# A Mamba mixer and a sorted mixture of experts: the state sums in two chains, the gate in one VectorE product

## What is computed

```python
def step(h, ins):
    d_t, B_t, C_t, u_t = ins
    dA = jnp.exp(d_t[:, :, None] * A)
    h = h * dA + (d_t * u_t)[:, :, None] * B_t[:, None, :]
    y = jnp.einsum('bds,bs->bd', h, C_t)
    return (h, y)
y = ys.transpose(1, 0, 2) + xm * D_ssm
y = y * jax.nn.silu(res)
return y @ out_w.T + out_b
```

## Time and profile before

| | us |
|---|---|
| three runs | 1684.01, 1685.93, 1693.28 |
| median | 1685.93 |
| span of the profiled execution | 1689.5 |
| of that, first product of the first slot to that of the last | 91.8 to 1573.7 |

### The profile page before, as it was taken

The page is one execution under the profiler, slowest core; times in us unless marked ns, Lnnn a source line. Parts: engine busy times, 40 slices in busy tenths (PEclk is TensorE's granted clock), DMA queues, the critical chain, the costliest instruction groups (busy, mean ns, idle before and its releaser), DMA issues. The chain is left out here.

```text
span 1689.5 us, 29263 instructions
## 1 busy us (share of the span) xinstructions
PE 1330.0 (79%) x8754; PEld 1198.4 (71%) x8754; DVE 1379.1 (82%) x2183; ACT 1278.8 (76%) x2660; POOL 572.0 (34%) x617
## 2 busy tenths in 40 slices
PE   7978568878887787878878787887878787568778
PEld 6867457768777686767767676777867676457668
DVE  3367888989888888989889898989889888988732
ACT  3489657978789787978779698878789698549722
POOL 1211423162423426162423536163332523132210
PEclk9988668988999899998999799998999899778889
DMA  7346446675666767676666767675676765455731
GB/s 233 112 95 136 85 83 149 152 169 126 156 158 139 166 142 180 142 170 134 146 159 142 162 146 165 142 179 125 136 175 141 163 148 114 92 129 126 161 88 45
DMA packets 144662, 236.98 MB, mean 140 GB/s; under 512 B 13696, under 2 KB 79488, under 8 KB 144384
## 3 DMA queue, kind: packets, MB, share of 16 engines
q0 software_dynamic: 39424, 132.15, 40.7%
q1 hardware_dynamic: 105088, 102.97, 20.8%
HBM read 92.46 MB, written 25.17 MB: 70 GB/s over the span
## 5 line engine op out<-in xcount | busy, mean ns | idle before, releaser
L1602 POOL DMA_DIRECT2D acc<-G x224 | 204.2, 911 | 855.8 <-DMA acc<-G 422.1
L973 ACT ACTIVATE dA<-delta,A 128x255 f32<-128x255 f32 x1024 | 425.6, 495 | 6.3 <-DVE hs L1344 5.3
L1350 DVE TENSOR_TENSOR_SCAN hs<-dA,b_r 128x512 f32<-128x512 f32 x256 | 297.9, 1202 | 19.9 <-PE b_r L660 12.6
L1363 DVE TENSOR_TENSOR G<-hs,b_r 128x1024 f32<-128x1024 f32 x224 | 272.4, 1216 | 44.8 <-PE b_r L671 34.9
L1344 DVE TENSOR_TENSOR_SCAN hs<-dA,dbu 128x1024 f32<-128x1024 f32 x128 | 292.8, 2287 | 15.1 <-ACT dA L973 8.8
L535 PE MATMUL b_h<-xsT,wst 128*128 128x128 f32 x1680 | 255.5, 301 | 34.4 <-issue 23.3
L535 PEld LDWEIGHTS b_h<-xsT,wst 128*128 128x128 f32 x1680 | 230.5, 212 | 50.7 <-issue 49.0
L547 PE MATMUL b_out<-w2s,hT 128*128 x1680 | 239.0, 289 | 13.5 <-ACT ys L894 9.6
L843 ACT ACT_TABLE_LOAD x182 | 233.5, 1283 | 4.0 <-PEq L1733 0.7
L547 PEld LDWEIGHTS b_out<-w2s,hT 128*128 128x128 f32 x1680 | 219.9, 203 | 18.4 <-issue 17.0
L660 PE MATMUL b_r<-prm,scaled 128*128 128x128 f32 x1024 | 173.5, 300 | 59.7 <-ACT scaled L989 28.8
(11 more groups left out here) (176 smaller groups left out, 1974.3 us busy)
## 6 DMA issues: line engine op xcount, KB each, us to landing
acc<-G POOLq DMA_DIRECT2D x224, 512.0 KB, 4.8
wst<-w_dram SPq DMA_DIRECT2D x242, 256.0 KB, 2.9
xsort<-sorted SPq DMA_DIRECT2D x70, 192.0 KB, 5.2
results<-ys SPq DMA_DIRECT2D x70, 192.0 KB, 3.0
xin<-x_dram SPq DMA_DIRECT2D x8, 256.0 KB
sorted<-ys SPq DMA_DIRECT2D x2, 960.0 KB, 7.3
sorted<-xn,posi POOLq DMA_INDIRECT x112
yk<-results,posi POOLq DMA_INDIRECT x112
```

The costliest lines, as they stand in the source:

```text
L973: last = do(dA[j % 4][:, d, k, 1:], delta[b][:, k, 1:], ACT.Exp, scale=A[:, k, s:s + 1])
L1350: V.tensor_tensor_scan(hs[j % 2][:, d, :, :].rearrange("p h t -> p (h t)"), dA[j % 4][:, d, :, :].rearrange("p h t -> p (h t)"), R[u % 2][ ...
L1363: V.tensor_tensor(to[:, :, :, :], hs[j % 2][:, :, :, :], both(C).unsqueeze(2).broadcast_to([P, DP, HALVES, T]), ALU.mult).then_inc(q_G, 1)
L1602: Q.dma_start(acc[b][:, :, :, :].rearrange("p d h t -> p (d h t)"), G[j % NG][:, :, :, :].rearrange("p d h t -> p (d h t)"), accum_op=ALU. ...
```

## The change

- `acc` gets the products 0, 2, 4 and 6, a new tile `odd` the products 1, 3, 5, 7 and D x. Products 0 and 1 are written by VectorE directly; 2 to 7 go through the ring of three. The even chain (q_even) and the odd chain (q_odd) wait for their own predecessor alone.
- GpSimd gets `skip` (two tensor_scalar of 128 x 256 that make D x, and a DMA that adds them to the first half of `odd`, 256 KB) and the merges `w1` and `w2` of the slot before: three tensor_tensor of 128 x 512. `w2` adds after the last landing twice in series.
- VectorE's gate is one product and waits for `w2`.
- `selr` holds one column for each selector (128 x 24) and the matmul reads it 128 times (a step of zero). It comes with the parameters; the three loads and the three casts of 128 x 1024 are gone, one cast of 128 x 24 remains.
- The lists of all four slots are in a new order on all four engines. In slot 0 TensorE has 14 pieces of an FFN and in slot 1 21, where there were 16 and 19. ScalarE's leaf F11 moves from slot 2 to slot 3.

```diff
+EVEN = (2, 4, 6)
+ODD = ("skip", 3, 5, 7)
...
     "vector": (
-        "b0 s0 g0 s1 gate g1 b2 s2 g2 s3 low b4 g3 delta s4 g4 s5 b6 mask g5 s6 g6 s7 xb g7",
-        "b0 fstats s0 s1 g0 fnorm b2 s2 flog ftop g1 fplace gate g2 s3 b4 xsum g3 un s4 g4 s5 g5 b6 fweights s6 "
-        "g6 low s7 delta g7 fsum",
-        "b0 s0 s1 g0 gate b2 g1 xsum s2 s3 un g2 b4 lx g3 s4 s5 g4 ln b6 low s6 g5 unx delta g6 s7 g7",
-        "b0 fstats s0 s1 fnorm b2 g0 flog ftop g1 fplace s2 g2 s3 gate g3 b4 s4 fweights g4 s5 low g5 b6 delta s6 "
-        "mask g6 s7 g7 xb fsum",
+        "b0 s0 g0 s1 gate b2 g1 s2 s3 low g2 b4 s4 g3 delta g4 s5 g5 b6 mask s6 g6 s7 xb g7",
+        "b0 fstats s0 s1 fnorm b2 g0 s2 flog ftop g1 fplace gate g2 s3 b4 xsum g3 un s4 fweights g4 s5 g5 b6 "
+        "s6 low g6 delta s7 g7 fsum",
+        "b0 s0 s1 g0 gate b2 g1 xsum s2 s3 un g2 b4 g3 lx s4 ln s5 g4 b6 g5 s6 low unx delta g6 s7 g7",
+        "fstats b0 s0 s1 fnorm b2 g0 flog ftop g1 fplace s2 s3 g2 b4 gate s4 fweights g3 g4 s5 g5 low delta "
+        "b6 s6 mask g6 s7 g7 xb fsum",
     ),
     "gpsimd": (
-        "a1 a2 a3 a4 a5 a6 a7",
-        "froot a1 sc0 sc1 sc2 a2 sc3 sc4 fkeep rms a3 sc5 sc6 sc7 rs a4 ga0 ga1 ga2 ga3 a5 ga4 ga5 ga6 ga7 a6 a7",
-        "a1 rms rs a2 a3 lnx rmsx a4 a5 a6 a7",
-        "froot a1 sc0 sc1 sc2 a2 sc3 sc4 fkeep a3 sc5 sc6 sc7 a4 ga0 ga1 ga2 ga3 a5 ga4 ga5 ga6 ga7 a6 a7",
+        "w1 w2 skip a2 a3 a4 a5 a6 a7",
+        "w1 froot w2 skip sc0 sc1 sc2 sc3 rms a2 sc4 sc5 a3 sc6 sc7 ga0 ga1 ga2 ga3 a4 a5 ga4 ga5 ga6 ga7 a6 "
+        "rs fkeep a7",
+        "w1 w2 rms rs skip a2 a3 lnx rmsx a4 a5 a6 a7",
+        "froot w1 w2 skip sc0 sc1 sc2 sc3 sc4 a2 sc5 sc6 a3 a4 ga0 ga1 ga2 sc7 a5 ga3 ga4 fkeep ga5 ga6 ga7 "
+        "a6 a7",
     ),
...
-        selr = sb("selr", [P, len(SELECTED), P], fp32r)
+        selr = sb("selr", [P, len(SELECTED)], fp32r)
...
+            def selector(row):
+                k = SELECTED.index(row)
+                return selr[:, k:k + 1].broadcast_to([P, P])
...
+        def landed(q, j):
+
+            if j in EVEN:
+                return q_even, 16 * (q * len(EVEN) + EVEN.index(j) + 1)
+            return q_odd, 16 * (q * len(ODD) + ODD.index(j) + 1)
...
-                if j:
-                    last = j - NG if j > NG else max(p for p in range(1, NP) if p % NG == j % NG) - (NP - 1)
-                    wait(dve, q_gs, (q * (NP - 1) + last) * 16)
-                to = G[j % NG] if j else acc[i % 2]
+                if j >= 2:
+                    wait(dve, *(landed(q, j - NG) if j - NG >= 2 else landed(q - 1, j - NG + NP - 2)))
+                to = G[(j - 2) % NG] if j >= 2 else (acc, odd)[j][i % 2]
...
             def gate_y(g, i):
                 q, b = 4 * g + i, i % 2
-                dve.wait_ge(q_gs, (q + 1) * (NP - 1) * 16)
+                dve.wait_ge(q_sum, 3 * q + 3)
                 dve.wait_ge(q_res, 2 * q + 2)
                 wait(dve, q_omm, q)
-                V.tensor_tensor(yg[:, :, :], acc[b][:, 0, :, :], acc[b][:, 1, :, :], ALU.add)
-                dve.drain()
-                for k in range(HALVES):
-                    V.scalar_tensor_tensor(out=yg[:, k, :], in0=xm[b][:, k, :], scalar=par("D_ssm")[:, k:k + 1],
-                                           in1=yg[:, k, :], op0=ALU.mult, op1=ALU.add)
-                dve.drain()
-                V.tensor_tensor(yg[:, :, :], yg[:, :, :], sres[b][:, :, :], ALU.mult).then_inc(q_yg, 1)
+                V.tensor_tensor(yg[:, :, :], acc[b][:, 0, :, :], sres[b][:, :, :], ALU.mult).then_inc(q_yg, 1)
...
                 pool.wait_ge(q_G, q * NP + j + 1)
-                wait(pool, q_gs, (q * (NP - 1) + j - 1) * 16)
-                Q.dma_start(acc[b][:, :, :, :].rearrange("p d h t -> p (d h t)"),
-                            G[j % NG][:, :, :, :].rearrange("p d h t -> p (d h t)"),
-                            accum_op=ALU.add).then_inc(q_gs, 16)
+                if j in EVEN:
+                    wait(pool, *(landed(q, j - 2) if j > 2 else landed(q - 1, 6)))
+                    Q.dma_start(flat(acc[b]), flat(G[(j - 2) % NG]), accum_op=ALU.add).then_inc(q_even, 16)
+                else:
+                    pool.wait_ge(*landed(q, j - 2 if j > 3 else "skip"))
+                    Q.dma_start(flat(odd[b]), flat(G[(j - 2) % NG]), accum_op=ALU.add).then_inc(q_odd, 16)
+
+            def skip(g, i):
+
+                q, b = 4 * g + i, i % 2
+                pool.wait_ge(q_xm, 2 * q + 2)
+                for k in range(HALVES):
+                    Q.tensor_scalar(xd[:, k, :], xm[b][:, k, :], par("D_ssm")[:, k:k + 1], 1.0,
+                                    ALU.mult, ALU.mult).then_inc(p_skip, 1)
+                pool.wait_ge(q_G, q * NP + 2)
+                wait(pool, *landed(q - 1, 7))
+                pool.wait_ge(p_skip, 2 * q + 2)
+                Q.dma_start(odd[b][:, 0, :, :], xd[:, :, :], accum_op=ALU.add).then_inc(q_odd, 16)
+
+            def merge(g, i, k):
+
+                q, b = 4 * g + i, i % 2
+                if k == 1:
+                    pool.wait_ge(*landed(q, 6))
+                    Q.tensor_tensor(acc[b][:, 0, :, :], acc[b][:, 0, :, :], acc[b][:, 1, :, :], ALU.add)\
+                        .then_inc(q_sum, 1)
+                else:
+                    pool.wait_ge(*landed(q, 7))
+                    Q.tensor_tensor(odd[b][:, 0, :, :], odd[b][:, 0, :, :], odd[b][:, 1, :, :], ALU.add)\
+                        .then_inc(q_sum, 1)
+                    pool.wait_ge(q_sum, 3 * q + 2)
+                    Q.tensor_tensor(acc[b][:, 0, :, :], acc[b][:, 0, :, :], odd[b][:, 0, :, :], ALU.add)\
+                        .then_inc(q_sum, 1)
```

More of the change, by code:

```diff
@@ L25 @@
         ("out_b_row", D), ("ident", P), ("dist", T), ("causal", T), ("iota", E), ("tap_b", DI), ("ones_row", P),
-        ("outside", PAD), ("before", P), ("steps", TILES), ("tiles", 15), ("ones_e", E)]
+        ("outside", PAD), ("before", P), ("steps", TILES), ("tiles", 15), ("ones_e", E), ("sel", 24)]
 DP = 2
@@ L156, with moe_mamba_kernel @@
     WIDTH += _w
-def moe_mamba_kernel(nc, x, pack, early, sel, w1, w2, out):
+def moe_mamba_kernel(nc, x, pack, early, w1, w2, out):
     fp32, fp32r, u32 = mybir.dt.float32, mybir.dt.float32r, mybir.dt.uint32
@@ L249, in moe_mamba_kernel @@
         acc = [sb(f"acc{b}", [P, DP, HALVES, T]) for b in range(SEQ)]
+        odd = [sb(f"odd{b}", [P, DP, HALVES, T]) for b in range(SEQ)]
+        xd = sb("xd", [P, HALVES, T])
         dtT = [sb(f"dtT{b}", [P, T + 2 * DS]) for b in range(SEQ)]
@@ L263, in moe_mamba_kernel @@
         SM = sb("SM", [P, T + P])
-        flat_in = [t[:, :, :, :].rearrange("p d h t -> p (d h t)") for t in (scaled[0], dA[0], hs[0], hs[1], G[0])]
-        win, taps, sel_in = flat_in[0], flat_in[1], flat_in[2:]
-        N_SEL = DP * HALVES * T
+        flat_in = [t[:, :, :, :].rearrange("p d h t -> p (d h t)") for t in (scaled[0], dA[0])]
+        win, taps = flat_in
         empty = ys
@@ L419, in _ @@
             sp.dma_start(taps, early[:, 3 * DI:]).then_inc(s_early, 16)
-            for b in range(NW, E):
+            for b in range(NW, E + 3):
                 whole_in(b)
-            for i, b in enumerate(sel_in):
-                sp.dma_start(b, sel[:, i * N_SEL:(i + 1) * N_SEL]).then_inc(s_sel, 16)
-                whole_in(E + i)
             sp.wait_ge(s_clear, 1)
@@ L427, in _ @@
             clear(xs_d[1])
-            for b in range(E + len(sel_in), STARTS):
+            for b in range(E + 3, STARTS):
                 whole_in(b)
@@ L652, in scan_input @@
                     for d in range(DP):
-                        last = mm(R[u % 2][:, d * T:(d + 1) * T], selr[:, SELECTED.index(DP * n + d), :], bcr[b][:, :],
+                        last = mm(R[u % 2][:, d * T:(d + 1) * T], selector(DP * n + d), bcr[b][:, :],
                                   start=True, stop=True)
@@ L670, in spread @@
                 for d in range(DP):
-                    last = mm(C[:, d * T:(d + 1) * T], selr[:, SELECTED.index(DS + DP * j + d), :], bcr[b][:, :],
+                    last = mm(C[:, d * T:(d + 1) * T], selector(DS + DP * j + d), bcr[b][:, :],
                               start=True, stop=True)
@@ L1110, in selectors @@
             def selectors():
[L1111 to L1114, removed]
+                V.tensor_copy(selr[:, :], par("sel"))
             def small_weights():
@@ L1579, in mixer_root, with flat @@
                 Q.tensor_scalar(xam[:, t, :], xa[:, t, :], 1.0, 0.0, ALU.mult, ALU.add).then_inc(g_xam, 1)
+            def flat(t):
+                return t[:, :, :, :].rearrange("p d h t -> p (d h t)")
             squares = []
@@ L1616, in slot @@
                         pair_sum(g, i, num)
+                    elif name == "skip":
+                        skip(g, i)
+                    elif name == "w":
+                        if tail:
+                            merge(*tail, num)
                     elif name == "sc":
@@ L1656, in finish @@
```

(9 more changed lines are left out.)

19 lines of the change are left out of this document (5 added, 14 removed), and 20 rows, old and new, of the table ORDER.

## The result

| | before | after |
|---|---|---|
| median, us | 1684.97 (1678.22 to 1693.28) | 1769.60 (1763.77 to 1774.62) |
| ratio | | 1.0487, 95% interval 1.0449 to 1.0525 |
| span profiled, us | 1689.5 | 1765.6 |

What follows compares the result with a forecast made beforehand. VectorE's queue was taken to set the pace of slots 0 and 2. Terms -55.4 - 13 + 14 + 9 = -45 us on a 1689.5 us span gave 1644, so about 1640 us expected; range 1610 to 1680.

Steps and rivals of the forecast that it cites:

- gate, less what ScalarE and TensorE take back: VectorE's gate: one product for four instructions, 1.73 us less in 32 slots, 55.4 us; ScalarE takes back 9 us.
- chain, columns and waits for `rstd`: Two chains of sums let `froot` run earlier: 13 of VectorE's 15.4 us of waits go; selector columns taken as no change.
- lock: New GpSimd operations hold up VectorE instructions over shared SBUF access: 0.45 us a slot, 14 us slower; ends 0 and 147.
- slot order: Steps move by one or two places on all engines: taken as 0, +-20 us.
- Rival A: ScalarE and TensorE take over in slots 0 and 2, so the gate gives only 14 us: 1668 us; chance 0.17.
- ScalarE's table loads: Two more table switches in a group, 16 x 1.28 = 21 us, in slot 3 where ScalarE idles: taken as 0.
- Selector columns: TensorE weight loads from one column read 128 times: no change taken; range -39 to +159 us of TensorE time.
- GpSimd: Merges, D*x products and one more DMA issue add 5.5 us a slot, 176 us in all, on an engine idle 66%.
- Rivals C: Late merges make the gate stall 4.5 us in 16 slots (0 and 2), 72 us: 1713 us; chance 0.08.
- D: Repeated-column weights load at twice the time, 5 us more TensorE in each slot: 1675 to 1690 us; chance 0.08.

Runs made afterwards that it cites:

- short gate alone: Kernel before with only the gate cut to one product, sum of the halves and D*x left out: 1671.90 us, 0.9891.
- one-column merges: New arithmetic in the old order, merges and, after the first slot, D*x on one column of each half only: 1647.96 us, 0.9740 against the kernel before.
- all old: New arithmetic with full-width merges, all engines' lists old, `w1 w2 skip` where `a1` stood: 1688.08 us, 0.9983 against the kernel before.

## Why the prediction was wrong

Forecast -45, measured +82. Ratios times 1686 us give, per step:

| step | forecast | measured | by |
|---|---|---|---|
| gate, less what ScalarE and TensorE take back | -46 | -18 | short gate alone |
| chain, columns and waits for `rstd` | -13 | -25 | one-column merges, less the short gate |
| lock | +14 | +41 | full against one-column merges |
| slot order | 0, +-20 | +85 | all new lists against all old |
| sum | -45 | +83 | |

The last three steps come from differences between neighbouring kernels, so the sum must close. By the intervals, the order's 85 is known to some 8 us, the others to 13 to 18 us each: the 25 of the chain is not told apart from the 13 forecast.

- **The step that failed is "the slot order itself moves steps by one or two places: without running it, +-20 us, taken 0".** It was a term put at nothing without a row to stand on, and it cost 85 us with the new arithmetic and 159 with the old. Nearly all of the cost of VectorE's list lies in slots 1 and 3, where VectorE was idle 8.9 and 9.3 us in the group of the earlier trace rows. That idle time could not be used freely: in slot 3 the late `g3` costs 1.0%; by the timeline it holds TensorE, TensorE holds ScalarE and so VectorE's `delta`, and TensorE's granted clock is lower. The diff shows such moves (`g3` behind `gate`, `s4` and `fweights`, while TensorE's `k4` needs it; `fweights` ahead of `g4` while the tanh had gone behind `turned`), but rows of before don't give their price: the second has the longest wait after, 51.9 us, and taking it away brought nothing. For slot 1 the cause stays open.
- **The gate** was cut as forecast (one product, 0.68 us, 32 times, no wait), but only a third of the 55 us stayed as gain: 37 were taken back where 9 were forecast. The mean slots of the kernel with the short gate alone are 0.4, 0.9, 1.1 and -0.1 us shorter than before, for 1.73 forecast in slots 1 and 3 and two thirds of it in 0 and 2. Rival A had the mechanism; its 14 us for the gate are near the 18 measured, though it gave slots 0 and 2 nothing and slots 1 and 3 half. VectorE's busy time fell by 48.3 us with the short gate alone (1379.1 to 1330.8), but by 8.9 in the kernel after, where its other instructions are some 39 us longer.
- **The chains**: waits for `rstd` and for the gathers fell by 14 and 34 us in the kernel after, as forecast or more; the time gained reads 25.
- **The lock** was undersized threefold. I counted scans of two SBUF inputs and spread the merges at random (chance 0.2); the list puts them always beside the same instructions, and `fnorm`'s operations with one input suffered most. One of the two readings behind the term was wrong too: in the earlier trace rows the scan at 1353.18 is released by ScalarE's dA, so it doesn't show GpSimd holding VectorE; the longer `fnorm` and scans do. The Trainium skill, SBUF — State Buffer, "Who interferes with whom", names `tensor_scalar`, copies and casts too among those that may take the shared ports. The trace agrees, with 756 against 339 ns; I had weighed only its half on two inputs.
- **ScalarE's table loads** rose by 16, 20.5 us, as counted; what they cost was not run apart. **Selector columns**: 0.3% faster by themselves (0.9950 to 0.9998), for nothing forecast. **GpSimd** got 201.7 us of work for the 176 forecast; merges take 1.27 us undisturbed and 1.50 on the mean.
- Rivals C (late gate: it never waits for a merge) and D (weight loads: 216 ns after) were both wrong in mechanism. No rival was "the order costs more than the rest brings", though it was the largest part of the diff.

Still open: which of slot 1's moves costs its 2.4%, what beside `g3` costs in slot 3, how much of the loss is TensorE's lower clock rather than idle time (its busy time rose by 27 us for the same 8754 matmuls), and whether the new lists with the merges behind `fnorm` gain as the old ones do.

## What to carry to other kernels

A reordering of in-order queues is no detail to be put at zero, least of all where an engine's idle time comes from waits for others that wait for it. Follow each moved step to what it waits for and to who waits for it; this shows where a delay can start, but not what it will cost, so run the order alone. When one wait is removed and the time stays, the slot is late for another reason; exchange whole lists and then slots to find it. Work given to GpSimd has its price by the VectorE instructions that stand beside it: moving it by one step cost 1.5% of this kernel, and making it wait for one step saved 1%.

## What the runs showed of the chip

- Beside GpSimd's two-input sums, VectorE's 128x128 `TENSOR_SCALAR` went from 339 to 756 ns on the mean, and one of 128x64 with two inputs from 226 to 1958 ns (one of them, 2.65 us long, ends at 732.48 as two merges of GpSimd end at 732.39). The 128x1024 scan with both inputs in SBUF went from 2294 to 2355 ns on the mean, the 128x512 scan with one of them in PSUM stayed at 1203 and 1201.
- GpSimd is held likewise: a sum of 1.27 us took 3.13 in the kernel after. It starts at 813.09, inside VectorE's scan with two SBUF inputs that runs from 812.20 to 815.16, and ends 1.06 us behind it. This scan in turn takes 2.96 us instead of 2.29; the GpSimd sum before, begun at 811.74, was still running when it started.
- TensorE's granted clock fell after idle time of TensorE. In slot 3 of the kernel after, by stretches of 4 us (columns as above):

```profile
884.00:888.00 4.00, 4.00 (x38) 3.94 (x36) 4.00 (x6) 2.90 (x6) 3.70 (x3) 1.00 0.52 115
888.00:892.00 4.00, 2.40 (x16) 1.81 (x14) 2.72 (x5) 3.80 (x8) 3.38 (x4) 1.00 0.76 170
892.00:896.00 4.00, 2.38 (x7) 1.92 (x8) 0.93 (x1) 3.69 (x11) 3.09 (x4) 0.55 1.10 251
896.00:900.00 4.00, 3.35 (x14) 2.64 (x13) 3.26 (x4) 2.56 (x6) 1.70 (x3) 0.50 1.02 262
```

Busy in full at 2.4 GHz, then 2.40 of 4 us busy, and the next stretches are granted 0.55 and 0.50, the 1.2 GHz level, in which 7 and 14 matmuls run for 38 before. TensorE's idle times there are 1.13 us for a product of VectorE and 2.09 us for ScalarE's `dtT`. Over groups 1 to 6 slot 1 has 0.84 after and 0.87 before, slot 3 0.88 and 0.99.
